# Last three residuals moved to VectorE, expert rows from the eighth group turned by VectorE and copied by ScalarE

## What is computed

```python
# block 1: three layers of a gated graph network
A = (adj != 0); h = layernorm(x)
for i in range(3):
    aggr = einsum('bst,bsd->btd', A, h @ weight[i])
    h = gru_cell(aggr, h)            # r, z sigmoid; n tanh; h = (1-z)*n + z*h
x = x + h
# block 2: one expert of 8 for each token
H = gelu(layernorm(x) @ W1 + b1)     # 128 -> 512
probs = softmax(H @ Wg + bg); e = argmax(probs)
x = x + probs[e] * (H @ Wd[e] + bd[e])
```

## Time and profile before

| | us |
|---|---|
| median of 3 runs | 542.11 |
| the runs | 538.12, 542.11, 544.45 |
| the profiled execution, device time | 537.82 |
| its span, first to last recorded instruction | 536.1 |

### The profile page before, as it was taken

The page is one execution under the profiler, slowest core; times in us unless marked ns, Lnnn a source line. Parts: engine busy times, 40 slices in busy tenths (PEclk is TensorE's granted clock), DMA queues, the critical chain, the costliest instruction groups (busy, mean ns, idle before and its releaser), DMA issues.

```text
span 536.1 us, 10215 instructions
## 1 busy us (share of the span) xinstructions
PE 485.8 (91%) x3048; PEld 392.9 (73%) x3048; DVE 358.3 (67%) x1151; ACT 318.3 (59%) x572; POOL 363.9 (68%) x352
## 2 busy tenths in 40 slices
PE   8999999999999999999989777977697998997983
PEld 4788888888878888888866545645386986986972
DVE  4788777998879888888789463835554552562532
ACT  3877977688667877878795553825342333333330
POOL 4489976999879988987777754554535462564555
PEclk9999999999999999999998897978788997997998
DMA  7512454112631111111210111113212323432110
GB/s 207 151 56 86 136 168 129 46 53 58 204 94 57 54 50 52 48 49 51 60 45 29 46 45 40 40 61 107 85 34 77 89 81 109 130 121 85 50 40 21
DMA packets 66341, 42.10 MB, mean 79 GB/s; under 512 B 9436, under 2 KB 61920, under 8 KB 66288
## 3 DMA queue, kind: packets, MB, share of 16 engines
q1 hardware_dynamic: 60464, 32.13, 20.8%
q0 software_dynamic: 4224, 8.92, 4.8%
q10 hardware_dynamic: 1600, 0.40, 0.3%
HBM read 16.90 MB, written 9.84 MB: 50 GB/s over the span
## 4 chain that ended last, share of the span: by engine, by line
PE 79%; issue 6%; DVE 5%; ACT 3%; another core or an unknown queue 2%; SPq 2%; DMA 0%; POOL 0%; POOLq 0%; DVEq 0%; ACTq 0%
PE bank L594 17%; PE bank L596 17%; PE bank L595 16%; PE bank L833 12%; PE bank L625 7%; PE bank L760 2%; ACT adj_i L1043 2%; PE bank L809 1%; PE bank L716 1%; PE bank L612 1%; PE bank L632 1%; SPq L358 1%; SPq L362 1%; ACT xn L950 1%
## 5 line engine op out<-in xcount | busy, mean ns | idle before, releaser
L1043 ACT ACTIVATE adj_i<-bank,b1c 128x512 f32<-128x512 f32 x132 | 86.0, 690 | 136.8 <-PE bank L596 75.6
L559 POOL DMA_INDIRECT sorted_rows<-xrow,pos x64 | 61.9, 967 | 54.8 <-issue 54.8
L459 POOL TENSOR_TENSOR diff<-hT,n_sb 128x512 f32<-128x512 f32 x48 | 68.2, 1420 | 16.8 <-ACT n_sb L932 16.7
L833 PE MATMUL bank<-wd_sb,adj_i 128*128 x512 | 65.8, 285 | 7.4 <-issue 6.1
L833 PEld LDWEIGHTS bank<-wd_sb,adj_i 128*128 128x128 f32 x512 | 62.7, 200 | 9.4 <-issue 8.9
L594 PE MATMUL bank<-hT_hi,w_hi 128*128 128x512 f32 x132 | 61.9, 469 | 5.1 <-issue 4.0
L461 POOL TENSOR_TENSOR diff<-z_sb,diff 128x512 f32<-128x512 f32 x48 | 62.5, 1303 | 3.8
L594 PE MATMUL bank<-ag_hi,wf_hi 128*128 128x512 f32 x144 | 58.9, 409 | 0.4 <-DVE ag_lo L1198 0.3
L595 PE MATMUL bank<-hT_lo,w_hi 128*128 128x512 f32 x132 | 56.7, 430 | 2.2 <-issue 2.1
L596 PE MATMUL bank<-hT_hi,w_lo 128*128 128x512 f32 x132 | 56.8, 430 | 0.8 <-issue 0.8
L595 PE MATMUL bank<-ag_lo,wf_hi 128*128 128x512 f32 x144 | 57.0, 396 | 0.0
(11 more groups left out here) (200 smaller groups left out, 1084.8 us busy)
## 6 DMA issues: line engine op xcount, KB each, us to landing
bands<-hT SPq DMA_DIRECT2D x192, 64.0 KB, 2.2
adj_i<-sorted_rows SPq DMA_DIRECT2D x64, 72.0 KB
xrow<-in_x_dram SPq DMA_DIRECT2D x16, 256.0 KB, 3.2
adj_i<-in_adj_dram SPq DMA_DIRECT2D x16, 256.0 KB, 3.6
sorted_rows<-xrow,pos POOLq DMA_INDIRECT x64
A<-wd_sb SPq DMA_DIRECT2D x4, 256.0 KB
hT<-wd_sb SPq DMA_DIRECT2D x4, 256.0 KB
sorted_rows<-padrow SPq DMA_DIRECT2D x9, 72.0 KB
```

The costliest lines, as they stand in the source:

```text
L459: nc.gpsimd.tensor_tensor(diff[:, b, :], hT[:, g, :], n_sb[:, b, :], ALU.subtract).then_inc(diff_ok, 1)
L559: nc.gpsimd.indirect_dma_start(out=sorted_rows, out_offset=bass.IndirectOffsetOnAxis(ap=pos[:, g, j:j + 1], axis=0), in_=xrow[:, g * GR + ...
L833: last = nc.tensor.matmul(o, HT[:, sg % 2, k, j * P:(j + 1) * P], wd_sb[:, bass.ds(at + k * P, P)], start=(k == 0), stop=(k == KC - 1))
L1043: nc.scalar.activation(HT[:, hb, k, 0:n], HB[k][:, 0:n], ACT.Gelu, bias=b1c[:, k:k + 1]).then_inc(done, 1)
```

## The change

It has two parts.

**Passage.** `residual` of the last three units (UN - 3, UN - 2, UN - 1) goes from GpSimd to VectorE, where it follows the transpose of that unit, and raises a new semaphore `x1_late`. VectorE's order becomes `step_gnn(UN)`, `residual(UN - 3)`, `gate_step(0)`, `gate_step(1)` with `step_gnn(UN + 1)` and `residual(UN - 2)` in it, `gate_step(2)`, `step_gnn(UN + 2)`, `residual(UN - 1)`. Statistics of groups 12 and 13 are both taken in `gate_step(1)`, those of 14 in `gate_step(2)`, those of 15 in `placed_first`; each is one gate step earlier than before (12 stays). GpSimd runs `row_scales(3)` directly after its `step_gnn(UN)`.

**Expert phase.** From the eighth group (BANDED = 7) on TensorE's four transposes go. VectorE normalises three groups ahead rather than two, turns 32x32 blocks of `xn` into `bands` (`row_blocks`), SyncE moves four blocks of 32 partitions from `bands` to `hn` (`rows_turned`, queued behind the next `load_rows`), ScalarE copies the high part from `hn`, and VectorE subtracts from `hn`. The columns of `hn` are in another order; the GELU writes them back in order through a rearranged view. `load_last` moves from SyncE's queue to ScalarE's, with the 16 register loads for its places.

```diff
+        BANDED = EARLY_SG + 1
@@ sync
+            def rows_turned(sg):
+                b, n = sg % 2, slots(sg) * SUB
+                sp.wait_ge(e_blk, sg - BANDED + 1)
+                hold(sp, e_xlo, sg - 1)
+                for q in range(QP):
+                    sp.dma_start(hn[:, b, q * n:(q + 1) * n],
+                                 bands[q * SUB:(q + 1) * SUB, b, 0:QP * n]).then_inc(e_col[b], 16)
...
             for sg in range(EARLY_SG, SGROUPS):
                 load_rows(sg)
-                if sg == EARLY_SG + 2:
-                    last_at = (places(mybir.EngineType.SP, wd_tab, SGROUPS - 1, (E - 1) * KC * P),
-                               places(mybir.EngineType.SP, bd_tab, SGROUPS - 1, (E - 1) * P))
-                if inside(sg - EARLY_SG - 2, GR * PIECES):
-                    load_last(sg - EARLY_SG - 2, *last_at)
+                if sg > BANDED:
+                    rows_turned(sg - 1)
+            rows_turned(SGROUPS - 1)
@@ gpsimd
-                if exists(u) and layer(u) == LAYERS - 1:
+                if inside(u, LATE_RESIDUALS) and layer(u) == LAYERS - 1:
                     residual(u)
...
-            for s in range(FIRST_STEPS, UN + 2):
+            for s in range(FIRST_STEPS, UN + 1):
                 step_gnn(s)
             row_scales(3)
-            step_gnn(UN + 2)
@@ tensor
-                if inside(s + 1, SGROUPS):
+                if inside(s + 1, BANDED):
                     turned_rows(s + 1)
@@ scalar
+            def slot_gelus(sg, chunks):
+                for k in chunks:
+                    hold(act, e_w1, sg * KC + k + 1)
+                    of = strip(HB[k][:], sg) if sg >= BANDED else by_slot(HB[k][:], sg)
+                    nc.scalar.activation(by_slot(HT[:, sg % 2, k, :], sg), of, ACT.Gelu,
+                                         bias=b1c[:, k:k + 1]).then_inc(e_h, 1)
...
             def expert_high(sg):
                 n = cols(sg)
-                act.wait_ge(e_t, sg + 1)
-                nc.scalar.activation(hT_hi[:, sg % 2, 0:n], pT[:, 0:n], ACT.Copy).then_inc(e_xhi, 1)
+                if sg < BANDED:
+                    act.wait_ge(e_t, sg + 1)
+                else:
+                    act.wait_ge(e_col[sg % 2], arrived(sg))
+                of = pT[:, 0:n] if sg < BANDED else hn[:, sg % 2, 0:n]
+                nc.scalar.activation(hT_hi[:, sg % 2, 0:n], of, ACT.Copy).then_inc(e_xhi, 1)
...
             def step(s):
                 hold(act, e_y, (s - 1) * GR)
-                gelus(s % 2, s, range(KC), e_w1, e_h, cols(s))
+                slot_gelus(s, range(KC))
                 if inside(s + 1, SGROUPS):
                     expert_high(s + 1)
+                k = s - EARLY_SG
+                if k == 0:
+                    act.wait_ge(tab_ok, 2)
+                    last_at.extend((places(mybir.EngineType.Activation, wd_tab, SGROUPS - 1, (E - 1) * KC * P),
+                                    places(mybir.EngineType.Activation, bd_tab, SGROUPS - 1, (E - 1) * P)))
+                if inside(k - 1, GR * PIECES):
+                    load_last(k - 1, *last_at)
@@ vector
+            def residual(u):
+                dve.wait_ge(hn_ok, u + 1)
+                gx = xres[:, graph0(u):graph0(u) + GR, :].rearrange("p g (i j) -> p g i j", j=QP)
+                tt(gx, gx, hn[:, u % 2, :].rearrange("p (g j i) -> p g i j", g=GR, j=QP), ALU.add).then_inc(x1_late, 1)
...
+                if s == 1:
+                    dve.wait_ge(x1_ok, GROUPS - QUAD + 1)
+                    for j in range(GR):
+                        last = gate_stats(GROUPS - QUAD, j)
+                    last.then_inc(g_bn, 1)
+                    late_stats(GROUPS - QUAD + 1, range(GR))
+                    gate_moments(GROUPS - QUAD)
+                    gate_moments(GROUPS - QUAD + 1)
...
+                if s == 1:
+                    step_gnn(UN + 1)
+                    residual(UN - 2)
...
+            def row_blocks(sg):
+                b, n = sg % 2, slots(sg)
+                dve.wait_ge(e_xn, sg * GR + n)
+                hold(dve, e_col[b], arrived(sg - 2))
+                nc.vector.transpose(bands[:, b, 0:cols(sg)].rearrange("p (j g t) -> p j g t", j=QP, t=SUB),
+                                    xn[:, b, 0:cols(sg)].rearrange("p (g i j) -> p j g i", g=n, j=QP)).then_inc(e_blk, 1)
...
             def step(s):
                 fine = s - 1 >= FINE
                 if inside(s + 1, SGROUPS) and not fine:
                     split_rows(s + 1)
-                if inside(s + 2, SGROUPS):
+                if inside(s + 2, BANDED):
                     rows_normal(s + 2)
+                if inside(s + 3, SGROUPS) and s + 3 >= BANDED:
+                    rows_normal(s + 3)
+                    row_blocks(s + 3)
...
             step_gnn(UN)
+            residual(UN - 3)
             gate_step(0)
             gate_step(1)
-            step_gnn(UN + 1)
             gate_step(2)
             step_gnn(UN + 2)
+            residual(UN - 1)
```

More of the change, by code:

```diff
@@ L286, in build @@
         FFN_WEIGHTS = UN - 9
+        LATE_RESIDUALS = UN - 3
         GATE_ROWS = UN - 7
@@ L321, in read, with arrived, strip, by_slot @@
             return 16 * sum(slots(n) * pieces(n) for n in range(sg % RING, sg + 1, RING))
+        BANDED = EARLY_SG + 1
+        def arrived(sg):
+            return sum(QP * 16 for k in range(BANDED, sg + 1) if k % 2 == sg % 2)
+        def strip(o, sg):
+            return o[:, 0:cols(sg)].rearrange("p (s g t) -> p s g t", s=QP, t=SUB)
+        def by_slot(o, sg):
+            return o[:, 0:cols(sg)].rearrange("p (g s t) -> p s g t", s=QP, t=SUB)
         def sent(n):
@@ L1038, in turned_high, with gelus @@
                 nc.scalar.activation(hT_hi[:, g % 2, :], pT[:], ACT.Copy).then_inc(g_xhi, 1)
-            def gelus(hb, s, chunks, ready, done, n=NT):
+            def gelus(hb, s, chunks):
                 for k in chunks:
-                    hold(act, ready, s * KC + k + 1)
-                    nc.scalar.activation(HT[:, hb, k, 0:n], HB[k][:, 0:n], ACT.Gelu, bias=b1c[:, k:k + 1]).then_inc(done, 1)
+                    hold(act, g_w1, s * KC + k + 1)
+                    nc.scalar.activation(HT[:, hb, k, :], HB[k][:], ACT.Gelu, bias=b1c[:, k:k + 1]).then_inc(g_h, 1)
+            def slot_gelus(sg, chunks):
[4 more added lines that the diff above has]
+                                         bias=b1c[:, k:k + 1]).then_inc(e_h, 1)
             HB = (pR, pZ, pGH, pGI)
@@ L1220, in state_rows, with late_stats @@
                     hold(dve, ag_ps, made("all", u + QUAD - 2) if layer(u - 2) < LAYERS - 1 else 0)
-                    hold(dve, x1_ok, made("last", u - 2))
+                    hold(dve, x1_ok, made("last", min(u - 2, LATE_RESIDUALS - 1)))
+                    if u - 2 >= LATE_RESIDUALS:
+                        dve.wait_ge(x1_late, u - 2 - LATE_RESIDUALS + 1)
                 nc.vector.transpose(hn[:, b, :].rearrange("p (g j e) -> p j g e", g=GR, j=QP),
                                     bands[:, b, :].rearrange("p (j g e) -> p j g e", g=GR, j=QP)).then_inc(hn_ok, 1)
+            def residual(u):
+                dve.wait_ge(hn_ok, u + 1)
+                gx = xres[:, graph0(u):graph0(u) + GR, :].rearrange("p g (i j) -> p g i j", j=QP)
+                tt(gx, gx, hn[:, u % 2, :].rearrange("p (g j i) -> p g i j", g=GR, j=QP), ALU.add).then_inc(x1_late, 1)
+            def late_stats(g, part):
+                dve.wait_ge(x1_late, g - QUAD * (QUADS - 1))
+                for j in part:
+                    last = gate_stats(g, j)
+                if part[-1] == GR - 1:
+                    last.then_inc(g_bn, 1)
             def normal_rows(u):
@@ L1520, in rows_normal @@
                 dve.wait_ge(e_in[r], read(sg))
-                hold(dve, e_t, sg - 1)
+                if sg - 2 < BANDED:
+                    hold(dve, e_t, sg - 1)
                 for j in range(slots(sg)):
```

39 lines of the change are left out of this document (20 added, 19 removed).

## The result

| | before | after | ratio, 95% interval |
|---|---|---|---|
| first chip, median us | 540.81 (534.36 to 544.52) | 548.90 (541.57 to 554.90) | 1.0136 [1.0104, 1.0168] |
| a second chip, median us | 475.28 (473.54 to 476.49) | 477.69 (476.86 to 478.77) | 1.0046 [1.0029, 1.0063] |

The change makes the kernel slower. The forecast was 536.5, in 529 to 545. On the first chip some executions fell in a slower state; the medians are over all of them, the ratio compares the fast ones alone. The profile shown ahead of the forecast and the profile after are from the first chip. No experiment ran there. They ran on three others (the second row of the table is one of them), on which the same kernel before takes 475.20, 475.28 and 475.15 us instead of 541; they are called the faster chips here.

A forecast was written before the change was run, and what follows sets the result against it. TensorE was taken as the bound, with 79% of the chain. Passage 1.5 plus expert phase 5.2 less a 1.1 stall gave 5.6 us, from a 542.1 median to 536.5, range 529 to 545.

The forecast's parts named there:

- The step that failed: Expert phase, SyncE's queue: four loads and four moves 3.6 us, register work 1.2, in a step of 7 us.
- Rival 3: Expert phase: row loads come too late for VectorE's rows_normal in every step, kernel slower, 550 us; chance 0.13.
- The transposes: Expert phase, TensorE: ten groups of four transposes removed, 0.44 us each by the chain, 4.4 in all; taken as 5.2.
- the wider pace of records: Expert phase, TensorE: eight records fewer per group save 0.5 to 0.7 us, so 5 to 7 us for ten.
- It has no deadline of its own here: Passage, GpSimd: losing three residuals of 1.62, 1.57 and 1.58 us is worth nothing.
- The late signal (rival 1): Expert phase: a late signal sets the pace, so removed transposes give nothing; 543 us; chance 0.25.
- The passage: VectorE between graph and expert phases: 3.5 us saved less added additions, net 1.5 to 2.1 us, taken as 1.5.
- the stretched operations: Passage, VectorE: three long operations, standing still while GpSimd adds, fall to usual length, saving 3.5 us.
- my upper price of 1.735: Passage, VectorE: added additions forecast at 0.68 us each; three at 1.735 would turn the gain into a 0.8 loss.
- The block transposes: Expert phase, VectorE: ten added, nearest row 0.70 us, at most 1.4 each, hidden behind its wait for e_y.
- The eighth group's stall: Expert phase: VectorE waits 3 us near 425 for the eighth group's rows; TensorE loses 0 to 2.5, taken as 1.1.
- ScalarE's 16 register loads and the weight transfers: Expert phase, ScalarE: loads some 0.2 us each and 16 transfers, hidden behind its copy in a 4.63 us wait.

The follow-up runs named there:

- experiment 7: Kernel before with three of TensorE's four transposes left out in each group from the eighth on, output not the reference's: 475.12 us, ratio 1.0001.
- experiment 8: Kernel before with three of four TensorE transposes left out from the eighth group on and GpSimd's second drain left out: 473.69 us, ratio 0.9953.
- experiment 9: Kernel before with only GpSimd's second drain left out: 475.90 us, ratio 1.0014.
- experiment 1: Kernel before with the passage part of the change alone: 475.28 us, ratio 0.9997.
- experiment 6: Changed kernel with its 40 moves issued by ScalarE instead of SyncE: 477.50 us, ratio 1.0049; another version, each move issued as two halves: 496.28 us, 1.0456.
- experiment 3: The changed kernel as it is, beside the kernel before on a faster chip: 477.69 us, ratio 1.0046.

## Why the prediction was wrong

**The step that failed** is the one on SyncE: its 40 added moves have no term in the sum, since four loads and four moves at 3.6 us and 1.2 of register work were to fit into a step of 7. On the faster chips it is 4.5 and 1.7, 6.2 in all. I took a move at the price of a row load (0.45 by the earlier trace rows); it takes 0.63. More than that, I set the sum against a step of 7 us, although my own forecast cut the undisturbed step to 6.3. A queue at 6.2 in a step of 6.38 is not hidden: it has lost its lead. And I treated all ten groups alike. The last one is fetched in eight pieces (5.26 us instead of 1.9, and 2.9 of register work ahead of them instead of 1.7). That its slots are halves stood in the text ahead of the forecast and in no term of my sum. In place of nothing the runs showed 1.0081 for the expert part alone, where 5.2 less 1.1 us had been forecast as a gain.

**Rival 3**, the slower one with a chance of 0.13, was the right mechanism: the row loads late for `rows_normal(s + 3)`, ahead of the output work, and TensorE waiting for the bias additions. It had the shape half right: VectorE waits 0.5 to 1.7 us in seven groups on a faster chip (on the first chip four waits, 11.8 us in all), but the quiet steps stay at 6.38, and only the 4 to 6 us at the last group reach TensorE, with the lowered clock behind them. Its bound was drawn at a landing time of 5 us; the last piece lands 1.9 us after its issue, and what ran out was the issuing time. SyncE's idle time, my reason for its low chance, had been given away by the change itself.

**The transposes.** By size the term was right: 0.44 us a group, and quiet steps of 6.38 where 6.82 stood. The forecast also took the wider pace of records and with it 5.2. No run shows that surplus. What was missing altogether is the other queue that ends level with TensorE. Of GpSimd the forecast said "It has no deadline of its own here", for the passage, and it looked no further, since the chain gave it 0%. The chain names the one queue that ended last, and not the one that ends just behind it. Whether GpSimd was level on the first chip is doubtful: the kernel before takes 66 us more there, and in its trace GpSimd waits up to 6.1 us for VectorE between its output scatters. So experiments 7 to 9 explain the faster chips.

**The late signal (rival 1)** is not needed on the faster chips: quiet steps shortened by the whole 0.44.

**The passage.** I wrote that the stretched operations end within 0.1 us of a residual; the first ends 0.15 after it. The three went as forecast; the additions cost 1.14 us each rather than 0.68, between that and my upper price of 1.735; it leaves about 1.2 of the 3.5. On the faster chips TensorE waits 1.08 and 1.25 us at these two places without the change (experiment 9) and 1.61 at the second alone with it (experiment 1), so some 0.7 us are left for it. Forecast 1.5, measured alone 0 (minus 0.6 to plus 0.8 us by the interval).

**The block transposes** at 1.10 us lie inside the bounds of 0.70 to 1.4. The Trainium skill, VectorE: DVE Perf Modes, section Rules for kernel authors, sends a 128x128 transpose to TensorE where its result may go to PSUM. The advice holds in this case: the time did not go to the blocks themselves, since with nine groups on VectorE and the last on TensorE the step still is 6.38, but to the moves that they need.

**The eighth group's stall** came: VectorE waits 3.06 us there on the first chip and 3.14 on a faster one, where 3 had been forecast at 425. The step takes 8.18 instead of 6.82, so 1.4 us against my 1.1. The working had an error that did little: the two answers of the earlier trace rows share one transfer, so twelve leave between 419.1 and 429.3, 0.85 us each, and not thirteen at 0.78. Likewise the matmul records of the three stretches are 355, not 354.

Timeline of VectorE, kernel after, first chip:

```profile
423.12 1.11 DVE L1589 TENSOR_SCALAR xn<-adj_i 128x128 f32<-128x128 f32 x4 [3.06 <-DMA adj_i<-sorted_rows]
```

**ScalarE's 16 register loads and the weight transfers**, "hidden": one step of 7.37 us on a faster chip falls where they stand, and the next is 5.59, so what was lost is given back. That they make the 7.37 is argued from their place. With the moves added to them (experiment 6) they no longer hide.

**What stays open.** The first chip loses 1.36%, a faster one 0.46%. The last group's stall is longer on the first (5.98 against 4.25), and SyncE's queue takes 7.49 us for the eight pieces instead of 5.26. The rest of the difference wasn't taken apart: no experiment ran on the first chip, so there the cause is read from one trace and not tested. On the faster chip the last group back on TensorE returns 1.6 of 2.4 us; the other 0.8 has no test. There too the chain between 380 and 440 us still lies for the most part on SyncE's queue.

## What to carry to other kernels

Before a queue is given more to issue, add up its whole step, issues at their own measured price and register work, and hold it against the step that the change itself makes shorter; then look at the group that is cut in more pieces than the others. After the run, ask for the chain in the phase that was changed, and not over the whole span: 15% there was nearly all of it here. Where a wait moves one step ahead on an engine, ask what stands behind it in its order: here a wait for input stood before the output work that frees TensorE's banks. And a chain shows one queue; ask of every other how much earlier it ends, because a gain on the first is worth only that much.

## What the runs showed of the hardware

One kernel takes 541 us on one chip and 475 on three others; the granted clock over the span is 0.95 in its profile on the one and 0.99 in the profiles of experiments 1 and 9 on two others. On the first chip there are stretches in which an engine's sequencer takes 0.7 us for each instruction. In the chain of the kernel after, SyncE's queue in such a stretch:

```profile
496.50 0.70 SPq L411
497.22 0.68 issue
497.92 0.74 SPq L411
```

Elsewhere the same issue takes 0.33 us and the pause 0.04. In the kernel before on that chip the register operations of the row loads take 37 ns in the median and up to 708; in experiment 3 none of the 72 takes more than 48. A stretch like this makes a serial queue longer. What causes it no run here shows, nor whether it makes the 66 us.

An addition of 128x512 on VectorE takes 0.68 us with its three operands in one layout, and 1.14 us when it adds `hn` into the rows of `xrow`. A `drain` of GpSimd kept it from its next transfer for 8.2 us when 88 indirect transfers had gone ahead and 3.2 us when 24 had (experiment 7; without that drain the same place takes 0.3, experiment 8). In experiment 3 TensorE's granted clock was 1.00 from 380 to 440 us and 0.52 for 5.8 us after it had stood 3.38 and 1.17 us; with the passage alone, without such waits, it stays at 1.00 up to 464.
